# Attention scores in 128 + 128 + 32 rows, with the last 32 rows of two units multiplied together

## The reference, cut to what matters

```python
hidden = concat([context, latents], axis=1)      # 2 x 1536 x 1024
q = latents @ Wq.T                               # 16 heads of 96
k = hidden @ Wk.T; v = hidden @ Wv.T             # 4 key/value heads of 96
scores = q @ k.T / sqrt(96)                      # each key head serves 4 query heads
out = softmax(scores) @ v
x = x + tanh(g_xattn[1]) * (out @ Wo.T)
```

## Time and profile before

| | |
|---|---|
| median of 3 runs | 1063.94 us (1063.51 to 1064.14) |
| the profiled execution | 1062.25 us, its span 1060.5 us |
| busy: PE, DVE, ACT, POOL | 1038.3, 641.5, 635.6, 644.3 us |
| granted clock of PE | 0.999 of full |

### The profile page before, as it was taken

The page is one execution under the profiler, slowest core; times in us unless marked ns, Lnnn a source line. Parts: engine busy times, 40 slices in busy tenths (PEclk is TensorE's granted clock), DMA queues, the critical chain, the costliest instruction groups (busy, mean ns, idle before and its releaser), DMA issues.

```text
span 1060.5 us, 18394 instructions
## 1 busy us (share of the span) xinstructions
PE 1038.3 (98%) x7262; PEld 586.4 (55%) x7262; DVE 641.5 (60%) x1092; ACT 635.6 (60%) x711; POOL 644.3 (61%) x348
## 2 busy tenths in 40 slices
PE   9999999999999999999999999999999999998987
PEld 4555444444545556566665655656656565565553
DVE  6989849644223565556556655654655655566767
ACT  5686535431224687665667756657766566677764
POOL 4476778242001589666677865668866667687771
PEclk9999999999999999999999999999999999999999
DMA  9986664843223999999999999899999999999995
GB/s 339 257 306 214 199 212 116 183 81 60 73 88 106 163 214 213 208 214 160 193 179 198 165 234 174 159 210 173 176 214 209 157 195 180 138 177 198 172 195 159
DMA packets 516570, 192.46 MB, mean 181 GB/s; under 512 B 484916, under 2 KB 500148, under 8 KB 516484
## 3 DMA queue, kind: packets, MB, share of 16 engines
q1 hardware_dynamic: 516484, 191.28, 87.5%
HBM read 56.88 MB, written 13.63 MB: 66 GB/s over the span
## 4 chain that ended last, share of the span: by engine, by line
PE 84%; DMA 4%; POOL 4%; DVE 3%; ACT 2%; issue 1%; SPq 1%; DVEq 0%; POOLq 0%
PE ps L556 34%; PE ps L798 20%; PE ps L772 11%; PE ps L813 10%; PE ps L815 5%; DMA region_o<-region_y 1%; DMA ln_t<-stage 1%; DVE p_max L1558 1%; POOL region_y L1723 1%; PE ps L578 1%; POOL x_res L1723 1%; POOL region_c L1723 1%; SPq L517 1%; DMA stage<-ctx_t_in 1%; POOL stage L1723 1%
## 5 line engine op out<-in xcount | busy, mean ns | idle before, releaser
L1723 POOL TENSOR_TENSOR region_y<-p,region_b 128x1536 f16<-128x1536 f32 x128 | 396.9, 3101 | 272.8 <-ACT region_b L1259 257.5
L1249 ACT ACTIVATE p<-ps,p_max 128x1536 f32<-128x1536 f32 x128 | 197.2, 1541 | 197.1 <-DVE p_max L1558 196.9
L1558 DVE TENSOR_REDUCE p_max<-ps 128x1 f32<-128x1536 f32 x128 | 224.9, 1757 | 113.8 <-PE ps L798 113.7
L798 PE MATMUL ps<-region_q,region_c 96*128 96x512 f16 x1152 | 269.8, 379 | 0.0
L813 PE MATMUL ps<-region_q,region_c 128*128 128x192 f16 x1536 | 207.6, 246 | 4.5 <-DVE logit L1583 2.4
L1259 ACT ACTIVATE region_b<-ps,p_max 128x1536 f16<-128x1536 f32 x128 | 196.5, 1535 | 18.5 <-DMA region_c<-region_b 17.8
L815 PE MATMUL ps<-region_q,region_o 128*128 128x96 f16 x1536 | 202.3, 206 | 0.0
L798 PEld LDWEIGHTS ps<-region_q,region_c 96*128 96x128 f16 x1152 | 105.3, 98 | 108.0 <-ACT region_b L1259 0.9
L813 PEld LDWEIGHTS ps<-region_q,region_c 128*128 128x128 f16 x1536 | 150.2, 98 | 23.1 <-issue 4.9
L815 PEld LDWEIGHTS ps<-region_q,region_o 128*128 128x128 f16 x1536 | 150.2, 98 | 13.2
L556 PE MATMUL ps<-region_w,region_q 128*128 128x512 f16 x576 | 134.9, 379 | 2.3 <-DMA region_q<-region_q 1.6
(11 more groups left out here) (151 smaller groups left out, 1152.7 us busy)
## 6 DMA issues: line engine op xcount, KB each, us to landing
stage<-ctx_in SPq DMA_DIRECT2D x16, 512.0 KB, 4.9
stage<-ctx_t_in SPq DMA_DIRECT2D x15, 512.0 KB, 8.7
stage<-wq_in SPq DMA_DIRECT2D x16, 384.0 KB, 4.1
stage<-wo_in SPq DMA_DIRECT2D x16, 384.0 KB, 4.3
k_scratch<-region_o SPq DMA_DIRECT2D x12, 384.0 KB, 6.8
region_q<-k_scratch SPq DMA_DIRECT2D x8, 576.0 KB, 5.9
region_q<-v_scratch SPq DMA_DIRECT2D x8, 576.0 KB, 6.2
x_res<-x_in SPq DMA_DIRECT2D x8, 512.0 KB, 8.8
```

The costliest lines, as they stand in the source:

```text
L798: ins = nc.tensor.matmul(bank(NSB * (m % 2) + sb_), q_head[0:HD, b, h, hq, qt * P:(qt + 1) * P], k_head[0:HD, b, hk, sb_ * 512:(sb_ + 1) * ...
L1249: nc.scalar.activation(p32[:, m % 2, :], rows, ACT.Exp, bias=p_max[:, m % 4:m % 4 + 1], accum_out=den[:, m % 4:m % 4 + 1]).then_inc(e32_ok, 1)
L1558: nc.vector.reduce_max(p_max[:, m % 4:m % 4 + 1], rows, axis=AX, negate=True).then_inc(max_ok, 1)
L1723: return nc.gpsimd.tensor_tensor(out, a, b, op)
```

## The change

In `scores`, the three passes over 96 rows are 288 rows of contraction, which are cut anew as 128 + 128 + 32.

- `q_head` and `k_head` now have 128 rows. In their rows 0 to 95 stands HI of the query in both planes (n = 0, 1) and HI and LO of the key; in rows 96 to 127 stand rows 0 to 31 and 32 to 63 of the low query, and of the high key. Two passes of three matmuls with 128 rows.
- The last 32 rows of the low query and of the high key (`q_rest`, `k_rest`) are held three times, at rows 0, 32 and 64. `score_rest` issues three matmuls of 32 rows, one for each bank, each from its own group of rows. From unit 2 on, an even unit issues its own three at its end and then, after a wait for `e32_ok` of the unit before, the three of the next unit; the odd unit then has only its six.
- `load_k` is five DMAs: the old one, one for rows 96 to 127 (2 x 32 x 1536) and three of 32 x 512 for `k_rest`.
- `take_q` writes the high half twice (1024 elements a row instead of 512). `take_low_q` writes the low query to `q_rest`; for stages 1 to 7 SP moves it: `spread_low_q` (two DMAs, in the unit after the last projection's end: unit 12, in stage 0 unit 9) and `copy_last_q` (two DMAs, in the next unit, behind a wait for the first two). For stage 0 DVE does it with copies, five for each projection and two more for the last.
- `p_hi` is now ACT's copy of `p32` (SBUF) and no second exponential of PSUM; ACT waits for its own `e32_ok` before it. So `scores` waits for `e32_ok` instead of `exp_ok`.

```diff
@@ -97,19 +98,23 @@
         ctx_t = view(region_c, 0, 16384).rearrange("p (b c h s) -> p b c h s", b=2, c=NC, h=2)
         w_eff = view(region_c, 0, 16384).rearrange("p (h c n) -> p h c n", h=2, c=NC)
 
-        q_head = view(region_c, 0, 8192).rearrange("p (b g h s) -> p b g h s", b=2, g=G, h=2)
+        q_head = view(region_c, 0, 8192).rearrange("p (b g n s) -> p b g n s", b=2, g=G, n=2)
         pt_hi = view(region_c, 8192, PT * SL).rearrange("p (r n q) -> p r n q", r=PT, n=NS)
         o_tok = view(region_c, 8192 + PT * SL, 2 * QG, F32).rearrange("p (r n) -> p r n", r=2)
+        q_low = view(region_c, 8192 + PT * SL + 4 * QG, QL)
         pt_lo = view(region_o, 0, PT * SL).rearrange("p (r n q) -> p r n q", r=PT, n=NS)
         p_hi = region_b[:, 0:SL].bitcast(F16).rearrange("p (r s) -> p r s", r=2)
 
         q2 = region_q[:, :]
-        k_head = view(region_q, 0, 4 * SL).rearrange("p (b h s) -> p b h s", b=2, h=2)
-        v_head = view(region_q, 4 * SL, 2 * NS * VW).rearrange("p (b s w) -> p b s w", b=2, s=NS)
-        o_t = view(region_q, 13824, 2 * 2 * QG).rearrange("p (r h j q) -> p r h j q", r=2, h=2, j=NJ)
-        v_last = view(region_q, 13824, 2 * KV * VW).rearrange("p (k t w) -> p k t w", k=KV, t=2)
-        o_cast = view(region_q, 15360, 2 * QG).rearrange("p (h n) -> p h n", h=2)
-        o_part = view(region_q, 16128, HD, F32)
+        k_head = view(region_q, 0, 4 * SL).rearrange("p (b n s) -> p b n s", b=2, n=2)
+        k_rest = view(region_q, 6144, 2 * QL).rearrange("p (b s) -> p b s", b=2)
+        v_head = view(region_q, 7168, 2 * NS * VW).rearrange("p (b s w) -> p b s w", b=2, s=NS)
+        o_t = view(region_q, 11776, 2 * 2 * QG).rearrange("p (r h j q) -> p r h j q", r=2, h=2, j=NJ)
+        v_last = view(region_q, 11776, 2 * KV * VW).rearrange("p (k t w) -> p k t w", k=KV, t=2)
+        o_cast = view(region_q, 13312, 2 * QG).rearrange("p (h n) -> p h n", h=2)
+        o_part = view(region_q, 14080, HD, F32)
+        q_rest = (stage[:, :, 3 * D // 4:D].bitcast(F16),
+                  view(region_q, 14272, G * QL).rearrange("p (g s) -> p g s", g=G))
 
         y_buf = region_y[:, :].rearrange("p (b d) -> p b d", b=2)
         p_lo = region_y[:, 0:SL].bitcast(F16).rearrange("p (r s) -> p r s", r=2)
...
@@ -304,6 +310,9 @@
 
         def q_end(m):
             return q_at(m)[0] if q_at(m) and q_at(m)[1] != 0 else None
+
+        def q_done(t):
+            return max(u for u, (j, part) in (Q_AT_FIRST if t == 0 else Q_AT).items() if j == NJ - 1)
 
         def wo_at(m):
             t, u = m // UPS, m % UPS
...
@@ -447,6 +456,11 @@
                 g, b = t // B, t % B
                 src = k_dram[b, :, g * HD:(g + 1) * HD, :].rearrange("h d s -> d h s")
                 sp.dma_start(k_head[0:HD, b, :, :], src).then_inc(k_ld[b], 16)
+                src = k_dram[b, HI, g * HD:g * HD + 2 * HP, :].rearrange("(n d) s -> d n s", n=2)
+                sp.dma_start(k_head[HD:P, b, :, :], src).then_inc(k_ld[b], 16)
+                for r in range(NSB):
+                    src = k_dram[b, HI, g * HD + 2 * HP:(g + 1) * HD, r * 512:(r + 1) * 512]
+                    sp.dma_start(k_rest[HP * r:HP * (r + 1), b, :], src).then_inc(k_ld[b], 16)
 
             def load_v(t):
                 g, b = t // B, t % B
...
@@ -489,6 +503,20 @@
             for s in range(RING):
                 load_wo(0, s)
 
+            def spread_low_q(t):
+
+                b = t % B
+                sp.wait_ge(q_free, 2 * NJ * (t + 1))
+                for n in range(2):
+                    sp.dma_start(q_head[HD:P, b, 0:NJ, n, :], q_rest[b][n * HP:(n + 1) * HP, 0:NJ, :]).then_inc(q_ld[b], 16)
+
+            def copy_last_q(t):
+
+                b = t % B
+                sp.wait_ge(q_ld[b], 64 * ((t + t % 2) // 2) - 32)
+                for n in range(2):
+                    sp.dma_start(q_rest[b][n * HP:(n + 1) * HP, :, :], q_rest[b][2 * HP:HD, :, :]).then_inc(q_ld[b], 16)
+
             def turn_o(k):
                 if k >= 2:
                     sp.wait_ge(wo_ready, 2 * k - 2)
...
@@ -511,6 +539,10 @@
                     turn_o(o_at(m))
                 if m - LAST in LOW4:
                     turn4(LOW4[m - LAST])
+                if t < TS - 1 and u == q_done(t) + 1:
+                    spread_low_q(t + 1)
+                if t < TS - 1 and u == q_done(t) + 2:
+                    copy_last_q(t + 1)
                 if m >= PT:
                     sp.wait_ge(pv_ok, m - PT + 1)
                 sp.wait_ge(exp_ok, m + 1)
...
@@ -784,19 +816,41 @@
                                  j == 0, j == NJ - 1)
                 ins.then_inc(wo_ready, 1)
 
+            def score_rest(m, start):
+
+                b, qt, h = m // UPS % B, m % UPS // G, m % G
+                for r in range(NSB):
+                    rows = slice(HP * r, HP * (r + 1))
+                    ins = nc.tensor.matmul(bank(NSB * (m % 2) + r), q_rest[b][rows, h, qt * P:(qt + 1) * P],
+                                           k_rest[rows, b, :], start=start, stop=not start)
+                return ins
+
             def scores(m):
 
                 t, u = m // UPS, m % UPS
                 b, qt, h = t % B, u // G, u % G
                 if u == 0:
-                    pe.wait_ge(k_ld[b], use(t, B))
+                    pe.wait_ge(k_ld[b], 5 * use(t, B))
+                rest_behind = m < 2 or m % 2 == 0
+                if m < G:
+                    pe.wait_ge(q_set, min(m + 1, NJ))
+                elif u == 0:
                     pe.wait_ge(q_free, 2 * NJ * (t + 1))
+                    pe.wait_ge(q_ld[b], 64 * ((t + t % 2) // 2))
                 if m >= 2:
-                    pe.wait_ge(exp_ok, m - 1)
-                for n, (hq, hk) in enumerate(((HI, HI), (HI, LO), (LO, HI))):
+                    pe.wait_ge(e32_ok, m - 1)
+                for n in range(2):
                     for sb_ in range(NSB):
-                        ins = nc.tensor.matmul(bank(NSB * (m % 2) + sb_), q_head[0:HD, b, h, hq, qt * P:(qt + 1) * P],
-                                               k_head[0:HD, b, hk, sb_ * 512:(sb_ + 1) * 512], start=n == 0, stop=n == 2)
+                        ins = nc.tensor.matmul(bank(NSB * (m % 2) + sb_), q_head[:, b, h, n, qt * P:(qt + 1) * P],
+                                               k_head[:, b, n, sb_ * 512:(sb_ + 1) * 512],
+                                               start=rest_behind and n == 0, stop=not rest_behind and n == 1)
+                if rest_behind:
+                    ins = score_rest(m, False)
+                    if m >= 2:
+                        if m + 1 < G:
+                            pe.wait_ge(q_set, min(m + 2, NJ))
+                        pe.wait_ge(e32_ok, m)
+                        score_rest(m + 1, True)
                 ins.then_inc(sc_ready, 1)
 
             def weigh(m):
...
@@ -913,7 +967,7 @@
                 if j == NJ - 1:
                     ins.then_inc(wo_ready, 1)
 
-            pe.wait_ge(exp_ok, NU - 1)
+            pe.wait_ge(e32_ok, NU - 1)
             pe.wait_ge(o_ok, NU - 4)
             turn_last(0, 30, (0, 1, 2))
             pe.wait_ge(fin_ok, 5)
...
@@ -924,7 +978,7 @@
             out_last(2, 30, 1, (0, 1))
             weigh(NU - 2)
             out_last(2, 30, 1, (2,))
-            pe.wait_ge(exp_ok, NU)
+            pe.wait_ge(e32_ok, NU)
             expert_mix(5, 3, 0)
             pe.wait_ge(o_ok, NU - 1)
             turn_last(4, 31, (0, 1))
...
@@ -1188,7 +1242,8 @@
                 if t >= B:
                     act.wait_ge(sc_ready, UPS * (t - 1))
                 for h, rows, part in q_rows(j):
-                    nc.scalar.activation(q_head[rows, t % B, h, HI, :], bank(at)[part, :], ACT.Copy, scale=SCALE
+                    both = bank(at)[part, :].unsqueeze(1).broadcast_to((part.stop - part.start, 2, 512))
+                    nc.scalar.activation(q_head[rows, t % B, h, :, :], both, ACT.Copy, scale=SCALE
                                          ).then_inc(q_hi, 1)
 
             def take_o(k):
...
@@ -1256,8 +1311,8 @@
                     take_q(NJ * (t + 1) + q_end(m), 7)
                 if m >= 2:
                     act.wait_ge(pt_hi_ld[(m - 2) % PT], use(m - 2, PT))
-                nc.scalar.activation(p_hi[:, m % 2, :], rows, ACT.Exp, bias=p_max[:, m % 4:m % 4 + 1]
-                                     ).then_inc(exp_ok, 1)
+                act.wait_ge(e32_ok, m + 1)
+                copy(p_hi[:, m % 2, :], p32[:, m % 2, :]).then_inc(exp_ok, 1)
                 if t % 2 == 0 and u in WO_SPLIT:
                     if t > 0:
                         act.wait_ge(wo_ready, 8 * t)
...
@@ -1539,11 +1594,32 @@
 
             def take_low_q(n, at):
                 t, j = n // NJ, n % NJ
-                for k, (h, rows, part) in enumerate(q_rows(j)):
-                    dve.wait_ge(q_hi, 2 * n + k + 1)
-                    nc.vector.scalar_tensor_tensor(q_head[rows, t % B, h, LO, :], bank(at)[part, :], SCALE,
```

(28 more changed lines are left out.)

4 lines of the change are left out of this document (3 added, 1 removed).

## The result

| | before | after |
|---|---|---|
| median | 1064.04 us (1063.51 to 1064.44, 4 runs) | 1056.17 us (1054.85 to 1057.24, 4 runs) |
| ratio, 95% interval | | 0.993 (0.9918 to 0.9942) |
| the profiled execution, its span | 1062.25, 1060.5 | 1056.73, 1055.0 |

A forecast was written before the change was run, and what follows sets the result against it. PE was taken to bound stages 1 to 6, with the DMA queue nearly full. Gains of 12.6 us there and 2.0 in stage 7 make 14.6, so 1047.6 profiled, 1049 median; range 1035 to 1062.

The forecast's parts named there:

- What bounds the kernel: Stages 1 to 6: PE full at 86.4 us a stage, each removed matmul worth 0.2167 until another wait ends last.
- A pair of units: Score matmuls on PE: a pair falls from 3.90 to 3.30 us, saving 0.60, or 4.8 a stage.
- `e32_ok` in unit 2: Second trio of unit 2 waits for unit 1's exponential: 0.5 us of stall a stage in stages 1 to 6.
- `take_q`: Its longer writes delay the bank for PE's side product: 0.4 us in units 6, 10 and 12, 1.2 a stage.
- The load in unit 1, and the low-query DMAs: Stages 1 to 6: extra key loads stall PE 1.0 us a stage; the four low-query DMAs are hidden at no cost.
- Sum of stages 1 to 6: A stage gains 4.8 - 0.5 - 1.2 - 1.0 = 2.1 us; six stages 12.6.
- Stages 0 and 7: Stage 0 gains zero, the full queue setting the pace from unit 6; stage 7 gains 2.0 us before the fourth block's transposes.
- 4.8 spare: After unit 11: four output units leave the queue 4.8 us spare, hiding the four low-query DMAs' 1.5 us and issues.
- The trios do not overlap: Rival in `score_rest`: six 32-row matmuls run in a row, 1.30 us, each pair loses 0.21; 1077 us, chance 0.15.
- The queue becomes the bound: Rival: 3 us of stall in unit 5, up to 1 after unit 12, stage 0 loses about 1; 1060 to 1063, chance 0.15.
- The queue has more room: Rival: the load's 1.0 us stall a stage goes and stage 0 yields 1; 1042 us, chance 0.18.

The follow-up runs named there:

- e9: Kernel after without the 128 DMA transposes of p_lo and the waits on them (stale low half): 1044.19 us, ratio 0.9819.
- e8: Kernel after, complete, with take_q writing plane 0 only and ACT copying it to plane 1 behind p_hi: 1049.27 us, ratio 0.9863.
- e11: Kernel after with the high query's second plane copied behind p_hi and the four extra key-row DMAs moved from unit 1 to unit 5, 9 or 7: 1043.52 us.
- e2: Kernel after with the four extra key DMAs of load_k left out from stage 2 on (stale rows): 1051.94 us, ratio 0.9887.
- e1: Kernel after without spread_low_q, copy_last_q and PE's wait for them (stale low queries in stages 1 to 7): 1054.90 us, ratio 0.9918.
- e13: Kernel after with stage 0 alone multiplying as before (nine 96-row matmuls, no joined groups, no DVE copies, no extra key rows): 1058.6 us, ratio 0.9949.
- e15: Kernel after with both stages 0 and 7 multiplying as before, stages 1 to 6 changed: 1057.03 us, ratio 0.9933.
- e16: Kernel after with the high query copied in two steps, extra key rows loaded later, and stage 0 as before: 1043.9 us, ratio 0.9815.
- e10: Kernel after without the low-query DMAs and, from stage 2 on, without the four extra key DMAs: 1047.81 us, ratio 0.9854.
- e14: Kernel after with stage 7 alone multiplying as before (96 rows, no joined groups, no low-query DMAs for it): 1056.25 us, ratio 0.993.
- e7: Kernel after with trios not joined in units 4, 10, 12 of stage 0, 2 of stages 1 to 6, 4, 8, 12 of stage 7: 1057.15 us.
- e6: Kernel after with unread matmuls filling PE's gaps in stage 0's unit 4 and before stage 7's router: 1056.84 us, ratio 0.9929.
- e17: Kernel after, complete, with stage 1's low queries placed by DVE copies during stage 0 instead of the four DMAs: 1074.36 us, ratio 1.0103.
- e12: Kernel after with the high query copied in two steps, extra key rows later, and unread matmuls in stages 0 and 7's gaps: 1048.91 us, ratio 0.9864.

## Why the prediction was right in the steady stages and failed in stages 0 and 7

**What bounds the kernel.** Right. PE was full at 86.4, and each matmul removed counted until another wait ended last.

**A pair of units.** Forecast 0.60 saved, measured 0.67. Two switches of 0.10 hold for 32 rows too. The trios cost 0.44 without the switch (0.54 - 0.10), where I had 0.49: the second trio does stand one pass behind the first, as I had it, but the step of 0.03 for the weight loads inside a trio is not there, as its three start within 0.02 us. By the Trainium skill's "TensorE: Matmul & The Clock Gate", section Measured speedup vs the span model, I had estimated 0.26 a trio. Here a trio takes 0.22, so three row tiles in a stream give nearly three times one pass; the trace is a little better than that estimate.

**`e32_ok` in unit 2.** Forecast 0.5 a stage, measured 0.57. In stages 1 and 5, whose unit 1 was late already, it is absent.

**`take_q`.** Forecast 0.4 in units 6, 10 and 12. Measured 0.37 each in e9 and in units 10 and 12 of after; unit 6 of after has up to 0.9, as its exponential is late by the queue. e8, which shortens `take_q` alone, removes those of units 10 and 12 from stage 2 on and leaves 0 to 0.8 in unit 6, of which the profile puts down the larger ones to transposes of p_lo; e11, which also moves the key rows, leaves 0 to 0.2. The mechanism is settled.

**The load in unit 1, and the low-query DMAs.** Forecast 1.0 of stall in unit 5. After has 0 to 1.0 in unit 5, and the load's delay also comes in unit 6. The waits of 1.70 and 1.30 in units 0 and 1 of stages 3 and 5 are not the load's: they stay in e2 (2.05 and 1.25, in unit 1 of both) and go in e1, so they come of the low-query DMAs of the stage before, which I had hidden at no cost. Together the queue costs 10.0 in six stages (after against e9), 1.7 a stage where I had 1.0; 1.45 of it was there before, as a wait in stage 1 (87.85 for 86.40). e2 gives back 4.7; e11, which also ends the waits for `take_q`, has stages 1 to 6 shorter by 8.0 in all.

**Sum of stages 1 to 6.** Forecast 12.6, measured 14.0: the larger saving (5.4 a stage for 4.8) was partly eaten by the larger queue cost.

**Stages 0 and 7: the step that failed.** It said 0 and -2.0; the profile has +6.4 and, with the stretch behind stage 7, +3.1. That is 11.5 us, more than the whole error.

*Stage 0.* The premise was wrong: "in stage 0 the full queue sets the pace from unit 6 on". Before, PE was busy for 82.78 of the 83 us of this stage, and its units 12 to 15 took 21.7 us, 0.2 more than their products:

```profile
333.00:416.00 83.00, 82.78 (x616) 48.60 (x615) 47.28 (x70) 60.11 (x69) 56.88 (x23) 1.00 1.02 197
```

Queue and PE were both full, and nothing had room. I set "0.75 MB more (2.5 us)" of queue against "at most 4.8 of PE" and called it zero; but where the transposes end last, what PE saves pays for nothing. e13 shows it: with PE's products as before, stage 0 is still 5.7 longer (4.6 in e15, whose stage 0 is the same). Of these 1.5 lie in units 6 and 9 (4.48 for 3.73 each), the `take_q` of stage 1's queries, which I had counted for steady stages only: e16, which splits it, has 3.73 in both. Another 0.6 in unit 10 is a wait for a transpose of p_lo that e15 does not have. The other 3.6 (3.1 in e15) lie in units 12 to 15, behind the low-query DMAs. The same four units take 24.9 in after and 21.5 in e1 and e10: these DMAs cost 3.4 there, and not nothing. I had hidden them under "4.8 spare" of output units, which at the end of stage 0, with its full queue, is not there.

In after itself the joined groups of units 4 and 12 come on top. Units 3 and 11 have no side product, and PE waits 1.92 and 1.10 for their exponentials, a wait that I had counted in unit 2 of the steady stages alone. Behind the first the clock is at half, which makes unit 4 another 1.64 longer. e9, without transposes of p_lo, has none of PE's waits on them in stage 0, and still takes 85.7. What is left there (us in total, times, longest; the first line is units 4 and 12, the second units 6 and 9):

```profile
PE ps L822 <- ACT p L1301: 3.6, 2, 1.9
PE ps L864 <- DVE region_c L1647: 2.2, 2, 1.2
```

So about half of the 6.4 is the queue's, and the rest comes of the joined groups, of `take_q` and of the clock, after all that PE saves.

*Stage 7.* I counted PE's saving until the fourth block's transposes take over. They had taken over from the start: from the scores of unit 15 of stage 6 to the router of unit 2 were 17.2 us before and 18.2 after. It is a chain of exponential, p_lo, normalisation and transpose that no matmul removed shortens. e14, with the old products in that stage, still has 84.5. e11, with the new ones, has 81.9, the 81.8 of before, and with the stretch behind it 123.9 for 124.7: a gain of 0.8 where I had 2.0. The rest of what after lost is for the most part the clock. PE's timeline in after and then in e11 (L588 and L595 are the side product, in units 2 and 13):

```profile
941.36 3.75 PE L588 MATMUL ps<-region_w,region_q 128*128 128x512 f16 x9
1002.77 3.71 PE L588 MATMUL ps<-region_w,region_q 128*128 128x512 f16 x9 [2.25 <-DMA region_q<-region_q]
...
930.28 2.11 PE L595 MATMUL ps<-region_w,region_q 128*128 128x512 f16 x9
989.70 2.10 PE L595 MATMUL ps<-region_w,region_q 128*128 128x512 f16 x9 [2.22 <-DMA region_q<-region_q]
```

The two units take 10.69 and 8.84 in after and 8.86 and 7.12 in e11, 3.5 of the 4.2 between the two stages. My forecast had no fall of the clock in it. This is one execution of each; the mean clock of the other runs (0.993 to 0.995 in after, 0.995 to 0.998 in e11) fits, but a link between it and the time of a run does not show.

**Why removing single causes returned so little.** This I can tell only in part. A wait that is taken away in one place comes back in another: in e1 in unit 5 of the steady stages (3.1 for 3.0), in e7 in unit 9 of stage 0. e2, e8 and e11, which take load or waits out of all stages, shorten the steady ones and keep it. e6 has stage 7 2.2 shorter and the same median, and its stages 1 to 6 are 2.2 longer for no reason that I know. That what counts is the queue and the waits over the whole run, and that the rest (e10's 8.4 against 1.3 + 4.2) comes of the same, is argued and not shown. Whether the low-query DMAs can be taken off stage 0's queue with profit stays open, as four of e17's copies stood beside POOL's subtraction and cost more than the DMAs.

**The rivals.** "The trios do not overlap" is disproved. "The queue becomes the bound" was right about the end of stage 0 and wrong about unit 5 of all stages, and its 1060 to 1063 was not reached. "The queue has more room" is false: the steady queue cost more than I had, not less.

## What to carry to other kernels

Account for each stage by its own bound, and look whether a second resource is full beside it: in stage 0 here PE and the queue both were, so the saving on one was worth little and what the change added to the other counted in full. Small DMAs that a change adds should go where the queue has the most slack, and an engine that frees a bank for another should do only what that bank needs (e11, which does both, gained 12.7 us over after with the same products and bytes). A group of small matmuls in separate rows of the array shares its two switches when several are joined: here 0.33 us saved a unit for 0.22 alone. Count the waits that the joining brings for every unit, not for the steady ones alone. And look which engines are busy beside a copy before pricing it by one that ran alone.

## What was not expected of the hardware

**The clock after a gap.** In unit 2 of stage 7 PE idles 2.86 us and then works at half the clock, 1.2 GHz; nine products take 3.75 instead of 2.11. After, PE's timeline and a window:

```profile
940.66 0.86 PE L588 MATMUL ps<-region_s,ln_t 128*128 128x64 f16 x24 [2.86 <-DMA ln_t<-stage]
...
942.00:944.00 2.00, 2.00 (x6) 0.67 (x5) 0.04 (x1) 1.91 (x3) 2.00 (x2) 0.50 1.14 211
```

The same happened behind the wait of stage 0's unit 4 (clock 0.50 from 358.5 to 360): it took 9.77 in after, and 8.13 in e1, e2, e9 and e10, which have the same wait of 1.92. In e11 a gap of 2.72 us before the router of stage 7 left its next nine products at 2.11, and in unit 13 a gap of 2.22 left full clock where one of 2.25 in after did not. So the length of the gap alone does not decide it. Filling the gaps kept the clock in the places that were filled and gained nothing (e6), and cost 5.4 on the best kernel (e12).

**A DVE copy of 32x512 took 0.28 us, or 3.14 to 3.16 beside POOL** (e17): into the same buffer, from the same source, by whether POOL's subtraction of 3.09 us was under way when it began.
